# Eight expert units from an early list right behind the last neighbour sums of a GNN and mixture-of-experts kernel, experts in descending order, x added one stage earlier

## What is computed

```
def sage(h, W_l, W_r, b):                       # neighbour mean and root term
    agg = segment_sum(h[src], dst) / max(deg, 1)
    return agg @ W_l + h @ W_r + b
x = x + sage(relu(sage(layernorm(x), W1_l, W1_r, b1)), W2_l, W2_r, b2)
t = layernorm(x)                                # tokens of the expert layer
p, e = top_k(softmax(t @ router_w.T), 2)        # 8 experts, 2 per token
p = p / max(p.sum(-1), 1e-12)
x = x + t + sum_k p[:, k] * (gelu(t @ w1[e_k] + b1[e_k]) @ w2[e_k] + b2[e_k])
```

## Time and profile before

| what | value |
|---|---|
| median of 3 runs | 594.65 us (593.85 to 594.86) |
| profiled execution | 592.88 us, span 591.2 us |
| PE busy | 554.3 us, 94% of the span |
| DVE, ACT, POOL busy | 364.7, 222.2, 185.5 us |
| mean granted clock of TensorE | 0.984 |

### The profile page before, as it was taken

One profiled execution on the slowest core, in us unless ns is written; L12 is line 12 of the kernel. 1 busy time (PEld: TensorE's weight loads), 2 busy tenths in 40 slices (PEclk: granted clock), 3 DMA queues, 4 the chain that ended last, 5 costly groups with the idle time before them and its releaser, 6 DMA issues.

```text
span 591.2 us, 11509 instructions
## 1 busy us (share of the span) xinstructions
PE 554.3 (94%) x3050; PEld 336.3 (57%) x3051; DVE 364.7 (62%) x1219; ACT 222.2 (38%) x422; POOL 185.5 (31%) x180
## 2 busy tenths in 40 slices
PE   4999999999999999999999999999991499999996
PEld 3555555555555555555445555555551488888885
DVE  5998667667657667663255766767678334444442
ACT  4676845434444434443101100000000155555554
POOL 3751000000000000000040154443356237787887
PEclk9999999999999999999999999999996799999999
DMA  8421211111111111012642146673332757787776
GB/s 259 148 79 60 65 45 54 48 34 54 44 37 55 37 44 54 28 55 53 196 129 80 55 137 200 202 245 126 106 130 97 228 109 118 125 142 129 129 116 92
DMA packets 64343, 61.24 MB, mean 104 GB/s; under 512 B 11281, under 2 KB 62334, under 8 KB 64302
## 3 DMA queue, kind: packets, MB, share of 16 engines
q1 hardware_dynamic: 47422, 44.84, 25.2%
q0 software_dynamic: 11200, 14.40, 13.1%
q10 hardware_dynamic: 5680, 1.49, 1.2%
HBM read 32.34 MB, written 29.30 MB: 104 GB/s over the span
## 4 chain that ended last, share of the span: by engine, by line
PE 69%; DMA 9%; DVE 8%; issue 8%; POOL 4%; SPq 1%; ACT 0%; POOLq 0%; DVEq 0%; ACTq 0%
PE bank L1306 22%; PE counts_ps L1448 8%; PE bank L1459 8%; PE bank L1221 8%; PE bank L1296 7%; PE counts_ps L662 7%; PE counts_ps L1306 4%; POOL xs_dram L593 2%; DMA rows<-in_x 2%; PE counts_ps L1439 2%; DMA xs_dram<-w,onehots 2%; DMA y<-y_dram 2%; PE bank L1211 1%; POOL stat L581 1%; PE bank L1289 1%
## 5 line engine op out<-in xcount | busy, mean ns | idle before, releaser
L1306 PE MATMUL bank<-y,adj 128*128 128x512 f16 x625 | 154.7, 379 | 0.4 <-ACT zt L1519 0.4
L1306 PE MATMUL counts_ps<-y,adj 128*128 128x512 f16 x625 | 144.0, 379 | 2.0 <-DMA y<-y_dram 2.0
L669 ACT ACTIVATE adj<-counts_ps 128x1000 f32 (+1 forms) x80 | 80.2, 1005 | 59.2 <-PE counts_ps L662 59.2
L635 POOL DMA_INDIRECT out<-adj x56 | 88.4, 1578 | 37.9 <-ACT adj L1654 18.5
L1306 PEld LDWEIGHTS counts_ps<-y,adj 128*128 128x128 f16 x625 | 60.7, 101 | 64.7 <-DMA y<-y_dram 4.3
L1306 PEld LDWEIGHTS bank<-y,adj 128*128 128x128 f16 x625 | 57.9, 97 | 59.5 <-issue 13.7
L565 POOL IOTA onehots<- 128x8 int32 x1 | 0.1, 143 | 225.4 <-PE counts_ps L662 225.4
L1448 PE MATMUL counts_ps<-adj 128*128 128x256 f32 x240 | 57.0, 380 | 0.0
L662 PEld LDWEIGHTS counts_ps<-onehots 125*128 125x128 f16 x640 | 42.4, 98 | 23.6 <-ACT adj L669 11.0
L648 DVE TENSOR_TENSOR onehots<-iota,lo_t 125x1024 f16<-125x1024 f16 x80 | 54.7, 684 | 1.8 <-issue 0.9
L1618 ACT ACTIVATE rows<-bank 128x256 f32<-128x256 f32 x25 | 9.6, 384 | 123.0 <-PE bank L1380 123.0
(11 more groups left out here) (237 smaller groups left out, 646.6 us busy)
## 6 DMA issues: line engine op xcount, KB each, us to landing
adj<-xs_dram SPq DMA_DIRECT2D x31, 264.0 KB
rows<-z_dram SPq DMA_DIRECT2D x49, 128.0 KB, 2.1
z_dram<-zt SPq DMA_DIRECT2D x33, 128.0 KB, 1.7
adj<-in_L_ffn_w SPq DMA_DIRECT2D x16, 256.0 KB, 3.2
rows<-in_x SPq DMA_DIRECT2D x24, 128.0 KB
out<-yo SPq DMA_DIRECT2D x24, 128.0 KB
y_dram<-yo SPq DMA_DIRECT2D x23, 128.0 KB, 1.7
y<-y_dram SPq DMA_DIRECT2D x4, 640.0 KB, 6.8
```

Of the source, the lines that this page charges most:

```text
L635: g.indirect_dma_start(out, bass.IndirectOffsetOnAxis(ap=ids[u][:, h:h + 1], axis=0), ye[u][:, h, :], None, bounds_check=N - 1, oob_is_err ...
L669: nc.scalar.activation(adj[:, :, bass.ds(at, GW * WD)].rearrange("p b (h d) -> p b h d", d=WD), counts_ps[:, 2 * (group % 2):2 * (group % ...
L1306: last = te.matmul(to, adj[:, b, t * P:(t + 1) * P], y[:, b, :], start=(b == 0), stop=(b == NT - 1))
```

## The change

It has these parts.

1. **x in layer 2's projection.** `split_y` adds the x row to the root row, with one more `tensor_tensor` behind a semaphore wait; SP loads the x row of the next tile in `rows_out` and that of the last tile behind the loop, in front of the chunk loads of `y`. `x2_and_var` loses one add and `node_tile` one load per tile, and `zx_taken` is now given after the first half of the sum.
2. **Order of the experts.** After tile 15 `order_experts` sorts the experts by their counts in the first twelve tiles, descending, and moves the counts so far along.
3. **The early list.** After tiles 18 and 19 `count_first` and `list_first` list eight full units made of rows of the first sixteen tiles; a small matmul in the sum of tile 21 spreads the list, `tables` writes it.
4. **Early units.** SP loads the rows of units 0 and 1 in the sum of tile 23, as soon as the scatters of tiles 0 to 15 have landed; `keep_meta` of both stands in front of the choice of batch 5. TensorE starts with unit 0 right behind the last sum. Eight units are written out one by one, and between them stand the turn, score, choice and placing of the last tile and batch, the filling of the ends, the list of the other 20 units (`list_rest`) and its spreading. ACT copies w1 of units 0 and 1. `FILLERS` goes.
5. **POOL's order.** The first two adds stand before the scatters of the last two tiles; the first 16 adds have no test of bounds.
6. `shares` has five instructions where seven stood, and can come later than the choice.

The core of the diff:

```diff
@@ SP: layer 1 @@
                 sp.dma_start(tile_rows(y2_dram, t), yo[:, :]).then_inc(S["y2_out"], 16)
+                sp.dma_start(xt[:, :], tile_rows(x, t + 1)).then_inc(S["x_in"], 16)
...
             root_rows(NT - 1)
+            sp.wait_ge(S["yz_in"], 2 * NT - 1)
+            sp.dma_start(xt[0:LAST, :], x[(NT - 1) * P:N, :]).then_inc(S["x_in"], 16)
...
@@ SP: layer 2 and experts @@
             def node_tile(t):
                 sp.wait_ge(S["zx_taken"], t + 1)
                 sp.dma_start(zi[:, :], tile_rows(z2_dram, t + 1)).then_inc(S["z_in"], 16)
-                sp.dma_start(xt[:, :], tile_rows(x, t + 1)).then_inc(S["x_in"], 16)
...
+            sp.wait_ge(S["table"], 1)
             first_row = row_of(0)
+            second_row = row_of(1)
+            sp.wait_ge(S["agg"], NT + EXPERT_END // P)
+            for q in range(2):
+                sp.wait_ge(scattered[q], 16 * TOPK * len(range(q, FIRST_OF[EARLY_BATCH], 2)))
+            load_rows(first_row, 0)
+            load_rows(second_row, 1)
+            sp.wait_ge(S["u_ready"], t + 1)
+            sp.dma_start(tile_rows(out, t), uo).then_inc(S["u_out"], 16)
...
+            row = row_of(6)
+            pad_expert(0)
+            pad_expert(1)
+            next_rows(6, row)
...
@@ POOL @@
+            for t, j in to_scatter[NT - BATCH - 1:FIRST_OF[NB - 1]]:
                 scatter(t, j)
             pool.wait_ge(S["table"], 1)
+            pool.wait_ge(S["u_out"], 16 * FIRST_OF[EARLY_BATCH])
+            for q in range(AHEAD):
+                add_half(0, q, True)
+            for t, j in to_scatter[FIRST_OF[NB - 1]:]:
+                scatter(t, j)
+            for q in range(AHEAD, EARLY_ROUNDS * HALVES):
+                add_half(q // HALVES, q % HALVES, True)
...
@@ DVE: split_y and x2_and_var @@
                 if bias is not None:
-                    last = v.tensor_tensor(root_to, of[:, D:2 * D], bias, ALU.add)
+                    dve.wait_ge(S["x_in"], 16 * (t + 1 - NT))
+                    link(v.tensor_tensor(root_to, of[:, D:2 * D], bias, ALU.add))
+                    last = v.tensor_tensor(root_to, root_to, xt[:, :], ALU.add)
                 last.then_inc(S["yz_in"], 1)
...
-                v.tensor_tensor(zt[:, :], zi[:, :], xt[:, :], ALU.add).then_inc(S["zx_taken"], 1)
-                dve.wait_ge(S["zx_taken"], t + 1)
                 dve.wait_ge(S["agg"], t + 1 + NT)
                 d = rdeg[:, bass.ds(t, 1)]
-                link(v.scalar_tensor_tensor(zt[:, :], counts_ps[:, s, 0:D], d, zt[:, :], ALU.mult, ALU.add))
+                v.scalar_tensor_tensor(zt[:, :], counts_ps[:, s, 0:D], d, zi[:, :], ALU.mult, ALU.add
+                                       ).then_inc(S["zx_taken"], 1)
...
@@ DVE: the new order @@
+            def early_unit(i):
+                dve.wait_ge(S["hid"], i - 1)
+                keep_w1(i, i % 2)
+                keep_meta(i, i % 2, 16 * (i // 2 + 1))
...
+                if t == FIRST_OF[SORT_BATCH] + BATCH - 1:
+                    order_experts()
+                if t == FIRST_OF[EARLY_BATCH] + 2:
+                    count_first()
+                if t == FIRST_OF[EARLY_BATCH] + 3:
+                    list_first()
                 if t % BATCH == 0 and 0 < j < NB - 1:
                     choose(j - 1)
                 if t == FIRST_OF[NB - 1]:
+                    keep_meta(0, 0, 16)
+                    keep_meta(1, 1, 16)
                     choose(NB - 2)
+            early_unit(2)
+            reached_by_batch()
+            early_unit(3)
+            choose_experts(NB - 1)
+            early_unit(4)
+            early_result(0)
+            shares(NB - 1)
+            place(NB - 1)
+            early_unit(5)
+            early_result(1)
+            list_rest()
+            early_result(2)
+            early_unit(6)
+            dve.wait_ge(S["listed"], 2)
+            tables(bank[0], NTAB, EARLY, NTAB, 2 * EARLY)
...
@@ PE @@
+            pe.wait_ge(S["sums_free"], NT)
             turn_rows(0, 16)
             turn_rows(1, 16)
+            pe.wait_ge(S["w1_in"], 2)
             hidden(0, 0)
+            pe.wait_ge(S["sums_free"], NT + 1)
+            hidden(1, 1)
             turn_rows(0, 32)
-            hidden(1, 1)
+            turn_token(NT - 1)
...
+            def early_round(i):
+                result(i, i % 2)
+                if i == 0:
+                    score(NT - 1)
+                if i == 1:
+                    prefix(NB - 1)
+                hidden(i + 2, i % 2)
+                turn_rows((i + 3) % 2, 16 * ((i + 3) // 2 + 1))
+            for i in range(4):
+                early_round(i)
+            list_units(spread, bank[0], 2)
+            for i in range(4, EARLY):
+                early_round(i)
...
@@ ACT @@
+            for i in range(EARLY):
...
+                gelu(i + 2, i % 2)
+                turn_rows(i + 3, (i + 3) % 2)
+                if i == 0:
+                    powers(NB - 1)
+                if i == 1:
+                    pad_experts(act, range(NE // 2, NE))
+                weigh(i, i // UNITS, i % UNITS)
```

More of the change, by code:

```diff
@@ L617, in _, with add_half @@
                     scatter(*to_scatter[t - BATCH - 1])
-            for t, j in to_scatter[NT - BATCH - 1:]:
+            def add_half(n, q, full):
+                u, h = q // 2, q % 2
+                before_it = pool.value_load(tab_wi[0:1, bass.ds(n * HALVES + q, 1)], min_val=0, max_val=2 * MAX_PAIRS)
+                pool.wait_ge(landed[q % NLAND], landed_before(n, q))
+                for d in range(1, NLAND):
+                    r = (q - d) % NLAND
+                    pool.wait_ge(landed[r], (before_it + (NLAND - 1 - r)) // NLAND * 16 + 32)
+                pool.wait_ge(S["ye_in"], n * HALVES + (q + 5))
+                pool.sem_inc(S["pool_held"], 1)
+                at = bass.IndirectOffsetOnAxis(ap=ids[u][:, h:h + 1], axis=0)
+                if full:
+                    g.indirect_dma_start(out, at, ye[u][:, h, :], None, compute_op=ALU.add).then_inc(landed[q % NLAND], 16)
+                else:
+                    g.indirect_dma_start(out, at, ye[u][:, h, :], None, bounds_check=N - 1, oob_is_err=False,
+                                         compute_op=ALU.add).then_inc(landed[q % NLAND], 16)
@@ new lines, in early_result @@
+            def early_result(i):
+                result(i, i // UNITS, i % UNITS)
+            for t in range(NT):
+                x2_and_var(t)
+                j = t // BATCH
+                if t % BATCH == 2 and 0 < j < NB - 1:
+                    place(j - 1)
+                if t == NT - 1:
+                    place(NB - 2)
+                if t == LIST_AT:
+                    dve.wait_ge(S["listed"], 1)
+                    tables(bank[2], EARLY, 0, EARLY, 0)
+                norm_and_sum(t)
+                if t == FIRST_OF[SORT_BATCH] + BATCH - 1:
[4 more added lines that the diff above has]
+                    list_first()
+                if t % BATCH == 0 and 0 < j < NB - 1:
+                    choose(j - 1)
+                if t == FIRST_OF[NB - 1]:
+                    keep_meta(0, 0, 16)
+                    keep_meta(1, 1, 16)
+                    choose(NB - 2)
@@ L1191, in _ @@
+            early_result(4)
+            dve.wait_ge(S["table"], 2)
+            for i in range(EARLY, EARLY + 3):
+                early_unit(i)
+                early_result(i - 3)
+            rounds = dve.value_load(nround_i[0:1, 0:1], min_val=MIN_ROUNDS, max_val=MAX_ROUNDS)
+            with dve.Fori(EARLY_ROUNDS, rounds) as n:
                 for u in range(UNITS):
@@ L1660, in _ @@
             gelu(0, 0)
+            gelu(1, 1)
             turn_rows(2, 0)
-            gelu(1, 1)
-            with act.Fori(0, rounds) as n:
+            phase3(NT - 1)
+            for i in range(EARLY):
+                if i + 2 == EARLY:
+                    act.wait_ge(S["table"], 2)
+                gelu(i + 2, i % 2)
[5 more added lines that the diff above has]
+                weigh(i, i // UNITS, i % UNITS)
+            rounds = act.value_load(nround_i[0:1, 0:1], min_val=MIN_ROUNDS, max_val=MAX_ROUNDS)
+            with act.Fori(EARLY_ROUNDS, rounds) as n:
                 for u in range(UNITS):
```

340 lines of the change are left out of this document (213 added, 127 removed).

## The result

The changed kernel takes 599.52 us in the median of 7 runs (598.9 to 601.41), the kernel before 594.86 us in the runs beside them: ratio 1.0085, 95% interval 1.0062 to 1.0108. Forecast were 582.5 us (575 to 590.5). The profiled execution has a span of 597.5 us where the one before had 591.2.

What follows compares the result with a forecast made beforehand. PE was taken as full but for a 27.4 us hole before the expert units, with POOL nearly as full; +6.3 +0.2 +1.4 -25.3 +4.95 +0.35 = -12.1 us, so 594.65 becomes 582.5 us, range 575 to 590.5.

Steps and rivals of the forecast that it cites:

- in the body of layer 1 it costs nothing: Layer 1's splits: the added x addition of 0.41 us on DVE costs nothing, as PE is the full engine.
- the chunk loads: Start of layer 2: the last x load delays the chunk loads of y and the first sum; with clock loss, +6.3 us.
- Lists and masks: Layer 2's sums: DVE's added list operations +0.2 us, masks of batch 5 late behind keep_meta +1.4 us.
- The term of 1.4 for rows that come late: Before batch 5's choice: keep_meta waits for rows of units 0 and 1, so PE waits longer for masks, +1.4 us.
- E' to the first result: From the end of the last sum (E') to the first expert result: 6.7 us instead of 31.98, so -25.3.
- The first five rounds: Early units: ACT's detours make PE wait 0.85 us before unit 4 and 3.15 before unit 5; +4.95 us in all.
- Part 5: Expert stage: POOL's row of adds, scatters and a landing sets the end, 126.9 us after the last sum; +0.35 us.
- E: Rival, chance 0.08: PE's clock stays low through layer 2's first sums; at three tiles 598.7 us, slower than before.
- C: Rival, chance 0.17: early stage runs at its slowest detour's pace, with POOL waiting for landings at expert changes; 587 to 592 us.
- B: Rival, chance 0.20: the early units' detours hide in ACT's idle time and POOL starts sooner; 577 us or a little under.
- D: Rival, chance 0.05: tile 15's scatter or the row loads land a tile later, moving the hole before the last sum; about 588.5 us.

Runs made afterwards that it cites:

- e5: Changed kernel, but x + b2 added in x's own buffer at the end of each tile, the split adding that sum: 590.27 us, ratio 0.9945.
- e9: Kernel before with one repeated VectorE addition of b2 in each split of layer 1, no transfer added or moved: 604.8 us, ratio 1.0192.
- e3: Changed kernel, layer 1's z1 loads issued ahead of stores and x load, last x load behind the five chunk loads: 595.08 us, ratio 1.0019.
- e6: Changed kernel with x + b2 added at the tile's end and the last x load behind the five chunk loads: 588.75 us, ratio 0.9911.
- e15: Changed kernel with x + b2 added at the tile's end and the last x load between second and third chunk load: 585.93 us, ratio 0.9847.
- e1: Changed kernel with its part 1 undone, x again loaded and added in layer 2: 584.92 us, ratio 0.9822 to the kernel before.
- e10: Changed kernel with x + b2 added at the tile's end and the last x load on ScalarE's queue: 588.9 us, ratio 0.9927.
- e12: Changed kernel with x as in e10, first four indirect adds brought forward and unit 1 weighed right behind the powers: 587.1 us, ratio 0.9902.
- e16: Changed kernel with x as in e15, early adds brought forward, ScalarE's fills on SP, result 3 ahead of unit 6: 589.86 us, ratio 0.9899.

## Why the prediction was wrong

- **Part 1, "in the body of layer 1 it costs nothing, since PE there is the full engine": this step failed.** It cost 10.25 us. That TensorE is busy all the time says that its suppliers come in time, not by how much. The one-hots came with no slack, behind the split in VectorE's order, and the split hangs on TensorE's own projection; 0.43 us in that chain are some 0.43 us per tile (e5, e9): 21 waits and 9.4 us over the whole of layer 1, in the kernel before one of 0.3. I asked what engine is full and should have followed what stands behind the added instruction.
- **Part 1, the chunk loads: right in mechanism, too small.** Idle 8.6 us where 6.8 were forecast; the first chunk came 6.3 us after its issue, where 4.5 had passed before (286.76 to 291.23). The clock took 2.5 us, not 0.5. Moving the load shows that both orders cost (e3, e6), and a place between the chunks doesn't (e15).
- **Lists and masks: forecast too high.** They were to cost 1.6 us; of the 3.0 in this stretch 2.5 are the clock's. The term of 1.4 for rows that come late didn't come: SP issued the loads of units 0 and 1 at 454.84, 10.4 us before E', no `keep_meta` waited for them, and TensorE waited 0.37 us for the last masks (464.73) where 0.29 were measured before.
- **E' to the first result: right**, 5.42 us for 6.7. The first five rounds: TensorE's unit 5 is 24.8 us behind unit 0 (470.62 to 495.41), 5.35 more than five undisturbed units of 3.89; forecast 4.95, with waits of 0.85 and 3.15 where 1.49 and 2.09 came.
- **Part 5: the right engine, 5.4 us too short.** Forecast 14.4 + 102.3 + 5.1 + 2.0 + 3.1 = 126.9 from E'; measured 15.1 + 102.7 + 5.15 + 3.6 (the landing before the 17th add) + 1.7 (two waits later, 1.26 and 1.08 for 0.30 each) + 4.1 (last add to the end) = 132.3. Two terms were mis-sized. The landing of 3.9 us was put for the whole interval in front of the 17th add, but it begins behind the add's 1.55 us. And 55 pitches of 1.86 leave out waits that the row had before, too: from 480.98 to 588.09 are 107.1 us, not 102.3.
- The forecast misses by 18.4: 10.25 + 1.8 (chunk loads) + 0.9 (sums, clock) + 5.4 (GpSimd).
- **Rivals.** E forecast slower, at 598.7, by a clock that stays low through layer 2; that didn't happen (1.00 from 316 us on), and that the time is so near is luck. E's price also put all 7.8 us of the hole's work into the 17 us at half clock; 5.35 of them lie there (449 to 466 us). C's landings are there (1.7 us), but that they stand at changes of expert isn't shown: they are at the 33rd and the 56th add, and the 33rd waited 1.39 us in the kernel before, too (544.89). B and D are out.
- The table loads: by the Trainium skill (ScalarE: Activation LUTs, "What ACT_TABLE_LOAD costs") a switch takes about 2.66 us. Here each takes 1.28, with no idle time before it, and the next activation follows at once (463.27 to 464.56, 479.85 to 481.14); the measurement decides.

The 1.5 us by which the row of adds is longer in e1 than in the changed kernel lie in the adds themselves: the last 40 are busy for 63.8 us, there for 62.3. Open: why some of them take longer, and how far GpSimd's row could be brought forward if no wait in the early units took its place.

## What to carry to other kernels

An engine at 100% does not by itself hide what you add on another: follow the chain from the added instruction to the next thing the full engine waits for, through every instruction that stands behind it in program order, and look for the slack there; if there is none, put the work at a point where its engine already waits. One small load beside a burst of large ones cost time on either side of it here (e5, e6); inside the burst, with part of it still to be issued, it cost none that e15 could measure. When the bound moves to an engine with a fixed row of work, as GpSimd's 56 adds, its first start and every wait inside that row are the whole budget, however early the results are.

## What the runs showed of the hardware

- A 128x256 f32 load issued behind (e3, e6), or on another queue beside (e10, e12), five chunk loads of `y` took 8.6 to 9.7 us to arrive; behind two of them 4.9 and 5.0 us (e15, e16).
- TensorE's granted clock at the boundary of the layers: 8.6 us of idle in the changed kernel were followed by 0.64 over the next 7 us. Shorter pauses went both ways. Idle of 2.03 and 0.78 us in e15 was followed by matmuls at half speed (3.62 us for four that take 1.88); 1.26 and 0.42 us in e1 left the clock at 1.00, and so did 2.84 and 0.41 us in e9 (the four take 1.88 at 304.96). These runs give no length of pause at which it falls.
